# A two-layer transformer kernel: projection parts made by other engines, routing spaced, exponentials taken by halves of the queries

## The reference, cut to what matters

```python
x = x + attn_a(layernorm(x))     # causal softmax(q k / 4) v, one k and one v for all heads
x = x + ffn(layernorm(x))
x = x + attn_b(layernorm(x))     # causal softmax(q k / 4 + slope * distance) v
x = x + ffn(layernorm(x))

def ffn(x):
    shared = (silu(x @ sw1.T) * (x @ sw2.T)) @ sw3.T
    scores = sigmoid(x @ router_w.T)
    top = top_k(scores + expert_bias, 2)
    share = scores[top] / (scores[top].sum(-1) + 1e-9)
    routed = sum(share[e] * (silu(h1_e) * h2_e) @ w3[e].T for e in top)
    return shared + routed
```

## Time and profile before

| | us |
|---|---|
| median of 3 runs | 1129.21 |
| lowest and highest | 1126.43 to 1132.49 |
| the profiled execution, its own time | 1143.65 |
| span of the profiled execution (first to last instruction) | 1141.8 |
| PE busy (matmul) | 1035.0, 91% of the span |
| PEld busy | 656.1, 57% |
| DVE busy | 790.4, 69% |
| ACT busy | 591.4, 52% |
| POOL busy | 404.2, 35% |

### The profile page before, as it was taken

How to read it: one execution, slowest core, us unless ns; L and a number is a source line. 1 busy time by engine, 2 the same in 40 slices (tenths; PEclk the granted TensorE clock), 3 DMA queues, 4 the chain that set the end, 5 groups by cost and what they waited for, 6 DMA issues and landing times. The chain is left out here.

```text
span 1141.8 us, 20106 instructions
## 1 busy us (share of the span) xinstructions
PE 1035.0 (91%) x6848; PEld 656.1 (57%) x6848; DVE 790.4 (69%) x1584; ACT 591.4 (52%) x1258; POOL 404.2 (35%) x426
## 2 busy tenths in 40 slices
PE   4799999999998898999887999999999887989998
PEld 3433333333376788888775343434334776888877
DVE  7898788887366754448687978887873757544465
ACT  6317677777743335533253367776676333355332
POOL 3503632323535215345553002321235442163361
PEclk9859999999998999999899799999999988999999
DMA  4550111110033224533149423332211421245351
GB/s 132 148 84 17 36 40 35 36 40 27 25 106 139 66 84 145 132 109 94 46 137 184 81 46 61 69 62 57 57 27 27 144 96 57 74 144 140 111 159 54
DMA packets 65380, 94.99 MB, mean 83 GB/s; under 512 B 20575, under 2 KB 49183, under 8 KB 62929
## 3 DMA queue, kind: packets, MB, share of 16 engines
q1 hardware_dynamic: 44549, 52.28, 17.7%
q10 hardware_dynamic: 13820, 22.54, 7.3%
q0 software_dynamic: 6912, 18.88, 6.3%
HBM read 66.33 MB, written 26.67 MB: 81 GB/s over the span
## 5 line engine op out<-in xcount | busy, mean ns | idle before, releaser
L1200 ACT ACTIVATE pt<-st_ps 128x512 f32<-128x512 f32 (+3 forms) x768 | 327.4, 493 | 187.8 <-PE st_ps L846 112.2
L846 PE MATMUL st_ps<-qs,ks 99*128 99x512 bf16 (+7 forms) x768 | 243.0, 330 | 8.0 <-ACT pt L1200 5.6
L1439 DVE TENSOR_REDUCE mab<-su_ps 128x1 f32<-128x512 f32 (+2 forms) x288 | 181.5, 662 | 28.1 <-PE su_ps L826 19.9
L603 POOL TENSOR_SCALAR_AFFINE_SELECT pt<-pt 128x512 f32<-128x512 f32 x112 | 71.1, 635 | 341.5 <-ACT pt L1200 341.5
L864 PE MATMUL o_ps<-pt,vp 128*32 128x512 f32 (+3 forms) x1536 | 163.6, 498 | 1.9 <-POOL pt L603 1.0
L822 PE MATMUL su_ps<-ks,qs 96*128 96x512 bf16 (+5 forms) x448 | 159.0, 370 | 2.9 <-DVE mab L1439 1.6
L846 PEld LDWEIGHTS st_ps<-qs,ks 99*128 99x128 bf16 (+1 forms) x768 | 73.3, 98 | 113.2 <-ACT pt L1200 63.3
L680 POOL DMA_INDIRECT rows_in<-rows,source x80 | 76.3, 954 | 154.0 <-PE st_ps L1037 70.2
L1226 ACT CAST hh<-hf 128x512 fp32r<-128x512 f32 x64 | 39.7, 620 | 168.7 <-DVE hf L1640 160.9
L178 PE MATMUL st_ps<-xt_h,wu 128*128 128x512 f32 x256 | 103.5, 404 | 6.3 <-DVE xt_l L1364 3.7
L179 PE MATMUL st_ps<-xt_h,wu 128*128 128x512 f32 x256 | 102.4, 400 | 0.0
(11 more groups left out here) (220 smaller groups left out, 2132.7 us busy)
## 6 DMA issues: line engine op xcount, KB each, us to landing
wu_raw<-w_units_dram SPq DMA_DIRECT2D x32, 384.0 KB
outs<-rows_out ACTq DMA_DIRECT2D x40, 256.0 KB
qs<-q_parts ACTq DMA_DIRECT2D x60, 128.0 KB
q_parts<-hml SPq DMA_DIRECT2D x16, 384.0 KB, 3.3
wexp_raw<-w_units_dram SPq DMA_DIRECT2D x16, 384.0 KB, 6.6
qs<-q_parts SPq DMA_DIRECT2D x36, 128.0 KB
inv<-inverses SPq DMA_DIRECT2D x128, 32.0 KB, 1.8
rows<-xn SPq DMA_DIRECT2D x8, 512.0 KB, 6.3
```

The source lines that it names most:

```text
L603: pool.affine_select(block, block, [[0, 4], [1, P]], ALU.is_ge, 0.0, base=0, channel_multiplier=-1).then_inc(masked, 1)
L846: last = pe.matmul(bank[KM_BANKS[n % len(KM_BANKS)]][:, lo - CH * part:hi - CH * part], key_stack(l, s)(j)[0:rows, P * kt:P * kt + P], qs[ ...
L1200: act.activation(pt[:, kt % 2, j, lo:hi], bank[KM_BANKS[i % len(KM_BANKS)]][:, lo - CH * part:hi - CH * part], ACT.Exp, scale=1 / np.sqrt( ...
L1439: dve.tensor_reduce(to, bank[SU_BANKS[n % len(SU_BANKS)]][:, 0:share * width].rearrange("p (j k) -> p j k", j=share), AX.X, ALU.max).then_ ...
```

## The change

1. **Blocks of exponentials.** `QUADS` takes all four blocks of the first half of the queries first, then the eight of the second half. The division of the previous step's results on POOL stands once, behind kt 3, instead of in two parts behind kt 2 and kt 4; in the last step POOL's other jobs stand there too.
2. **Output projections.** In the last step they stand behind pieces 2, 5, ..., 23 instead of 10, 13, ..., 31, and those of the tiles 8 to 11 behind pieces 40, 42, 44 and 46 instead of behind the transposes after attention.
3. **Routing and searches.** The stages are spread over later items, the low parts of the two experts' weights go behind items 12 and 14.
4. **Projection parts.** ACT's float32 copy `yb` goes (32 rows of it stay for layer 0's keys and values); DVE subtracts the high part straight from PSUM, and the cast of the second part goes to ACT (`middle`). In layer 0 the transposes of a chunk stand inside the groups of the one ahead.
5. **Layer 1's last chunk.** All six groups of chunk 3, four splits among them, stand in the prelude, behind maxima 2, 5, ..., 17.
6. **Opening.** The filled part of `vp` is 128x1024 instead of 128x8192, and chunk 0's first rows are normalised right behind their own statistics.
7. **Between attention and feed forward.** DVE's order changes (the normalisation of chunk 2 ahead of the second division), and POOL's last weight split waits until all rows are normalised.

```diff
-ROUTE_BEHIND = {2: (0, 1), 3: (2, 3), 4: (4, 5), 8: (6,), 9: (7,)}
-FIND_BEHIND = {5: (0, 1), 6: (2, 3), 7: (4, 5)}
+ROUTE_BEHIND = {3: (0,), 4: (1,), 5: (2, 3), 6: (4, 5), 10: (6,), 11: (7,)}
+FIND_BEHIND = {7: (0, 1), 8: (2, 3), 9: (4, 5)}
-EXPERT_BEHIND = {4: 6, 6: 7}
+EXPERT_BEHIND = {12: 6, 14: 7}
...
-QUADS = [(kt, part) for kt in range(QT) for part in range(kt // HALF, 2)]
+QUADS = [(kt, 0) for kt in range(HALF)] + [(kt, 1) for kt in range(QT)]
...
-FC_BEHIND = {10 + 3 * t: t for t in range(QT)}
+FC_BEHIND = {**{2 + 3 * t: t for t in range(QT)}, **{40 + 2 * t: QT + t for t in range(HALF)}}
-INVERT_AT, DIVIDE_BEHIND = (6, 27), (2, 4)
+INVERT_AT, DIVIDE_BEHIND = (6, 27), 3
...
-FIRST_UNITS = {2: 4, 3: 8, 4: 12, 5: 16}
+FIRST_UNITS = {0: 2, 1: 5, 2: 8, 3: 11, 4: 14, 5: 17}
...
-                        elif s and kt in DIVIDE_BEHIND:
-                            divide(l, s - 1, DIVIDE_BEHIND.index(kt))
+                        elif s and kt == DIVIDE_BEHIND:
+                            divide(l, s - 1, 0)
...
-                if kt == 0:
+                if kt == 3:
                     split_unit(l, 0)
-                if kt == 1:
                     divide(l, STEPS - 2, 0)
-                if kt == 2:
                     split_unit(l, 1)
-                if kt == 3:
                     divide(l, STEPS - 2, 1)
-                    rstds(2 * l + 1, 0, 1)
-                if kt == 4:
-                    rstds(2 * l + 1, 1, 2)
+                    rstds(2 * l + 1, 0, 2)
 
...
+                rstds(2 * f + 1, 2, 3)
                 split_unit(f, 2)
-                rstds(2 * f + 1, 2, 4)
+                rstds(2 * f + 1, 3, 4)
+                pool.wait_ge(xn_done, TT * (2 * f + 2))
                 split_unit(f, 3)
...
-                transpose_chunk(0, 1)
-                pe.wait_ge(w_split, 2)
                 for c in range(NCH):
+                    if c == 0:
+                        pe.wait_ge(w_split, 2)
                     pe.wait_ge(xtl_done, KE * (c + 1))
-                    for m in range(3):
-                        qkv_group(0, c, m)
-
+                    qkv_group(0, c, 0)
+                    if c + 1 < NCH:
+                        transpose_chunk(0, c + 1)
+                    qkv_group(0, c, 1)
+                    qkv_group(0, c, 2)
                     n = qkv_index(0, c, 0)
-                    pe.wait_ge(evac_done, n + 1)
+                    pe.wait_ge(kv_copied, c + 1)
+                    pe.wait_ge(rest_done, split_index(0, c, 0) + 1)
                     for t in range(TC):
                         last = pe.transpose(bank[4 + n % 4][:, 32 * t:32 * t + 32],
-                                            yb[0:32, split_index(0, c, 0) % 2, P * t:P * t + P], ident[0:32, 0:32])
+                                            yb[0:32, c % 2, P * t:P * t + P], ident[0:32, 0:32])
                     last.then_inc(vt_done, 1)
-                    if c + 2 < NCH:
-                        transpose_chunk(0, c + 2)
 
...
                 transpose_chunk(p, 0)
                 transpose_chunk(p, 1)
-                for tt in range(QT, QT + HALF):
-                    output_projection(l, tt)
                 route(l, 0)
                 route(l, 1)
...
+                        last.then_inc(values_taken, 1)
+                    else:
+                        y = split_index(l, c, m)
+                        bias = {"bias": bias_a[:, m:m + 1]} if l == 0 else {}
+                        wait(act, parts_out[y % PBUFS], 16 * (y // PBUFS))
+                        act.activation(hml[:, y % PBUFS, 0, :], src, ACT.Identity, **bias).then_inc(high_done, 1)
+                        if kind == "kv":
+                            wait(act, vt_done, c - 1)
+                            act.activation(yb[0:32, c % 2, :], src[0:32, :], ACT.Identity, bias=bias_a[0:32, m:m + 1]).then_inc(kv_copied, 1)
+                            if c + 1 < NCH:
+                                x_hi(0, c + 1)
+                    if cast is not None:
+                        middle(cast)
+                    cast = y if kind != "v" else None
+                    if (l, c, m) == (1, 0, 5):
+                        x_hi(2, 2)
+                    if (l, c, m) == (1, 2, 1):
                         x_hi(2, 3)
+                if cast is not None:
+                    middle(cast)
 
+            def middle(y):
+                act.wait_ge(rest_done, y + 1)
+                act.copy(hml[:, y % PBUFS, 1, :], yr[:, y % 2, :]).then_inc(mid_done, 1)
 
...
-            act.activation(vp[:, :, :, :].rearrange("p t h d -> p (t h d)"), mhalf[:, 0:1].to_broadcast([P, TT * H * 32]),
-                           ACT.Identity, scale=-2.0).then_inc(ones_set, 1)
+            act.activation(vp[:, :, 0:H // 2, :].rearrange("p t (o j) d -> p t o j d", o=2)[:, :, :, 0, :],
+                           mhalf[:, 0:1].unsqueeze(2).unsqueeze(3).to_broadcast([P, TT, 2, 32]), ACT.Identity, scale=-2.0).then_inc(ones_set, 1)
...
-                dve.wait_ge(evac_done, qkv_index(l, c, m) + 1)
+                src, high = qkv_bank(qkv_index(l, c, m)), hml[:, y % PBUFS, 0, :]
                 dve.wait_ge(high_done, y + 1)
+                if l == 0 and m == 0:
+                    dve.wait_ge(kv_copied, c + 1)
                 wait(dve, parts_done, y - 1)
-                dve.tensor_tensor(yr[:, y % 2, :], yb[:, y % 2, :], hml[:, y % PBUFS, 0, :], ALU.subtract).then_inc(rest_done, 1)
-                dve.wait_ge(rest_done, y + 1)
-                dve.tensor_copy(hml[:, y % PBUFS, 1, :], yr[:, y % 2, :]).then_inc(mid_done, 1)
-            def split_chunk(l, c):
-                for m in range(SPLIT[l]):
-                    split(l, c, m)
                 if l == 0:
-                    n = qkv_index(l, c, 0)
-                    dve.wait_ge(vt_done, c + 1)
-                    src = bank[4 + n % 4][:, 0:32 * TC].rearrange("p (t m) -> p t m", m=32)[:, :, D:32]
-                    dve.tensor_copy(vp[:, TC * c:TC * c + TC, 0, 0:D], src)
-                    dve.tensor_copy(vp[:, TC * c:TC * c + TC, 4, D:32], src).then_inc(vc_done, 1)
+                    dve.scalar_tensor_tensor(yr[:, y % 2, :], src, bias_a[:, m:m + 1], high, ALU.add, ALU.subtract).then_inc(rest_done, 1)
+                else:
+                    dve.tensor_tensor(yr[:, y % 2, :], src, high, ALU.subtract).then_inc(rest_done, 1)
...
             def qkv_b():
+                split(1, 0, 0)
                 add_shared(0, 2)
-                split(1, 0, 0)
+                split(1, 0, 1)
                 stats(2, 2)
-                split(1, 0, 1)
+                split(1, 0, 2)
+                add_shared(0, 3)
+                split(1, 0, 3)
                 normalise(2, 2)
-                split(1, 0, 2)
-                split(1, 0, 3)
-                split_chunk(1, 1)
+                split(1, 1, 0)
+                stats(2, 3)
+                split(1, 1, 1)
+                split(1, 1, 2)
+                normalise(2, 3)
+                split(1, 1, 3)
                 lows(2, 2)
-                add_shared(0, 3)
-                stats(2, 3)
                 split(1, 2, 0)
-                normalise(2, 3)
                 split(1, 2, 1)
+                lows(2, 3)
                 split(1, 2, 2)
                 split(1, 2, 3)
-                lows(2, 3)
-                split(1, 3, 0)
-                split(1, 3, 1)
...
             def attention(l):
                 for u in range(NSU - 1):
-                    if l and u - 2 in (FIRST_UNITS[2], FIRST_UNITS[3]):
-                        split(1, 3, 2 if u - 2 == FIRST_UNITS[2] else 3)
+                    for m in range(SPLIT[1]):
...
                 stats(p, 1)
+                invert(step_no(l, STEPS - 1), 0)
                 normalise(p, 0)
-                invert(step_no(l, STEPS - 1), 0)
                 normalise(p, 1)
                 divide_last(l, 0)
+                add_projection(l, 4)
+                add_projection(l, 5)
+                stats(p, 2)
                 lows(p, 0)
                 invert(step_no(l, STEPS - 1), 1)
                 lows(p, 1)
-                add_projection(l, 4)
-                add_projection(l, 5)
-                stats(p, 2)
+                normalise(p, 2)
                 divide_last(l, 1)
                 hidden(l, 0)
-                normalise(p, 2)
                 hidden(l, 1)
                 add_projection(l, 6)
...
```

100 lines of the change are left out of this document (57 added, 43 removed).

## The result

The changed kernel takes 1145.97 us (median of 4 runs, 1144.12 to 1146.24) where the kernel before, in 4 runs beside it, takes 1130.84 (1126.43 to 1132.49): a ratio of 1.0137 with a 95% interval of 1.0103 to 1.0170. It is slower by 1.4%; the forecast was 1118.5, in a range of 1104 to 1132. A ratio leaves out a run that stands far above the others of its kernel (one of the four of experiment 15, 2411.68 us).

A forecast was written before the change was run, and what follows sets the result against it. PE was taken to bound the steps with maxima, with gains only in its gaps elsewhere. 14 + 6 - 11.1 - 9.2 - 3.5 - 7 = -10.8 us; -10.7 from the median 1129.21 gave 1118.5, range 1104 to 1132.

The forecast's parts named there:

- Blocks by halves, steps with maxima: Fourteen attention steps with maxima: exponentials' buffers wanted again sooner, 1.0 us lost a step, +14 us, bounds +4 to +27.
- the prediction's own sign: The prediction called itself wrong if the steps alone differ from +14 by over 10, or ACT holds up the projection.
- PE's own work per block: Attention steps: PE's work shared by a block's queries plus 128, 3.04 us for 512, 2.43 for 384, 1.83, 1.22.
- Rival (b): Attention steps: each of eight tight blocks costs 0.3 us or more, 2.3 a step, +42 instead of +20, 1140; chance 0.12.
- Last step: Last attention step of each layer: the buffer cycle sets the pace, projections mostly hidden; +3.0 us each, +6 together.
- Between: Between attention and feed forward: projections leave, 2.8 us a layer, and normalisation avoids POOL's weight work; -11.1, bounds -7 to -14.
- Routing: First feed-forward items: DVE's routing work moved to later items, -5.1 us in layer 0, -4.1 in layer 1; -9.2 together.
- rival (d): First items and projection: closing PE's gaps keeps the clock at 2.4 GHz, perhaps 7 us more gain, 1111; chance 0.08.
- Opening: Start to first scores: smaller fill on ACT and earlier first normalisation, 10.64 to about 7.9 us; -3.5, bounds -1 and -6.
- Which move with it: Opening: the rest of the chain to the first scores at 49.45, parts, stores and loads, moves with the first normalisation.
- Projection and prelude: Layer 1's projection and prelude: DVE loses casts, gain taken as nearly PE's 6.4 us of idle time; -7 us.
- The rule of the Trainium skill on VectorE's copies: Float32 SBUF copies run at 2x on VectorE, not with PSUM operands; if so here, projection gain some 5 us smaller.

The follow-up runs named there:

- experiment 15: Changed kernel, two buffers, with the old order of the blocks, old POOL divisions and projection places, low parts ahead of additions; ratio 0.9899 to the kernel before.
- Experiment 4: Changed kernel with a third buffer of exponentials for the second half of the queries, instruction order untouched; 1116.15 us, ratio 0.9881 to the kernel before.
- experiment 14: Kernel before with the third buffer for the second half of the queries, old order of the blocks; ratio 0.9900 to the kernel before.
- Experiment 2: Kernel before with the new order of the blocks alone; ratio 1.0292 to the kernel before, 33 us slower.
- experiment 11: Kernel of experiment 9 with the four projections behind the transposes and DVE's low parts ahead of their additions; ratio 0.9826 to the kernel before.
- experiment 12: Kernel of experiment 9 without POOL's wait for the normalised rows ahead of its last weight split; ratio 0.9895 to the kernel before.
- experiment 6: Kernel before with the new places of routing stages, searches and two experts' low parts alone; ratio 0.9888 to the kernel before, 11.7 us less.
- experiment 8: Kernel of experiment 7 with layer 0's opening reordered too: POOL's later roots behind last parts, DVE's chunk 0 splits earlier; 1117.64 us, ratio 0.9893.
- Experiment 7: Third-buffer kernel of experiment 4 with layer 1's projection reordered, POOL's first last parts ahead of roots and DVE's splits earlier; 1112.79 us, ratio 0.9844.
- experiment 9: Kernel of experiment 7 with two of chunk 3's groups and their splits back ahead of layer 1's prelude; 1108.09 us, ratio 0.9805 to the kernel before.
- experiments 3 and 10: Changed kernel with old block order and four projections behind the transposes, ratio 1.0098; kernel of experiment 9 with those four projections behind the transposes, 0.9889.

## Why the prediction was wrong

The sum failed by 25.9 us (-10.8 forecast, some +15 measured). By its own steps:

**Blocks by halves, steps with maxima: +14 forecast, +29.6 measured.** This step decided, and by the prediction's own sign (over 10 from +14) it failed. The mechanism was right: ACT waits for values at 8 places, and the cycle of a tight wide block is 3.14 to 3.16 us where I had 3.12. What failed is the other side of the comparison, "PE's own work per block". I spread the maxima evenly and got 3.04 for a block of 512. Experiment 4 shows 2.85, 3.07, 2.45 and 2.55: units are whole, and some wide blocks get few. So four wide gaps cost 12.32 - 10.92 = 1.4 us, where I had 0.24 for three. The pair at the end of a step costs 0.58, but did so before (experiment 14), and this I had misread too: that PE doesn't wait there was read from PE's idle time, which lists no wait for exponentials in layer 0's seven steps (0.30 us of idle time in a steady step, and 0.35 with the third buffer, when these 0.58 are gone). The stretch 78 to 287.6 that I divided by seven isn't the seven steps either: these run from 72.63 to 279.34. With both, a period pays 1.98 for two buffers against 0.58 in the old order, and 0.35 more since by halves it runs at 29.51 and not at 29.16 with three: 1.98 - 0.58 + 0.35 = 1.75, the measured difference of periods. The 0.35 is about the one wait of 0.30 that PE has for ACT's exponentials in the first half, which keeps its two buffers in experiment 4; under the old order with three (experiment 14) PE has no such wait in these steps. No run gives the first half a third buffer, so that this is the cause is likely and not shown. I had 0.7 for these two blocks.

The period is that of layer 0. Over the seven steps, the old order with three buffers takes 203.62 and 204.90 us and halves with three take 206.00 and 214.46: of the 29.6 us, 2.4 in layer 0 and 9.6 in layer 1 are left when the second half's reuse is gone, and some 18 are that reuse. Layer 1's 9.6 stay open. PE waits there for ACT for 5.7 us in 15 places, and under the old order not at all; the seven steps of layer 1 took 212.9 to 218.2 in the seven profiles by halves with three buffers, and 204.6 and 204.9 in the two of the old order. Rival (b), 2.3 a step, was the nearest to the truth, and I gave it 0.12. I had its evidence: PE stands in order, and a sum of small shortfalls has no slack to be paid from where PE is full.

**Last step: +6 forecast, +9.8 measured.** Experiment 2 has +2.0 from the blocks in each; the other 2.9 are the projections (3.0 by experiment 11), of which I had hidden all but 1.7.

**Between: -11.1 forecast, -12.6 measured.** The size is right. The move of the four projections takes 3.9 and 3.8 out of this stretch (experiment 11), but nearly all of it comes back in the last step: together it is worth 0.9 in layer 0 and nothing in layer 1. The normalisation beside POOL is real: 1.0 and 4.3 by experiment 12. These are 13.1 already, so nothing is left for DVE's new order by itself.

**Routing: -9.2 forecast, -12.6 to item 10 and -15.6 to item 15 measured;** alone -12.4 to item 15 (experiment 6). DVE was what the items waited for. The rise of the granted clock from 0.85 to 1.00 in this stretch, half of rival (d), is part of it: at 2.4 instead of 1.2 GHz PE's own work is shorter (busy 37.26 us with 197 matmuls before, 33.57 with 208 now), which my count of DVE's work left out. How much of the gain is the clock's no run separates. The Trainium skill ("TensorE: Matmul & The Clock Gate", Part 1) has idle gaps bring the lower clock. The traces agree: PE's longest gaps in this stretch of layer 0 were 3.65 and 2.60 us before, at a clock of 0.85, and are 1.75 and 1.41 now, at 1.00.

**Opening: -3.5 forecast, +0.5 measured,** which is no change: with this opening the first scores come at 49.5 to 50.1 us in the other profiles (experiment 8 aside, which changes it), with the old one at 49.5 to 49.8. The first normalisation starts at 8.29 us (10.64 before, 7.9 forecast). Nothing of it arrives at the first scores: PE waits 8.03 us for the stack (4.21 before), which comes from the last parts. "Which move with it" was the wrong step: the first last part starts at 24.15 us, 23.34 before, and the sixth ends at 36.5, 36.3 before. Why is argued only. POOL takes the roots of all four chunks ahead of its first last part and waits 3.75 us for the last chunk's statistics, but experiment 8, which moved these roots, changed other things with them and lost.

**Projection and prelude: -7 forecast, +3.5 measured.** DVE did lose its work (31.39 to 20.45 us busy), and POOL's parts take 1.17 instead of 1.55. But I bounded the gain by PE's idle time, and the stage ends with a chain: DVE's difference, ACT's cast, POOL's part, a store and a load. In it POOL first waited 11.02 us for statistics. Experiment 7 took 4.1 us off by order alone. In the prelude the two more groups cost 1.4 to 1.6 (experiment 9). The rule of the Trainium skill on VectorE's copies that the prediction weighed changed nothing: neither engine's load set this stage's end.

So four of six sizes lay outside their bounds, two of them with the wrong sign, and the one that decided was the cover I computed from an even spread instead of reading it.

## What to carry to other kernels

When a change brings the reuse of a buffer nearer, compare its cycle with the work that the waiting engine has between exactly these uses, block by block, and not with the average; on an engine that is full every shortfall is lost, and its idle time doesn't show it: of 1.75 us more in a step, PE's idle time showed 0.7. Only the distance between the same instructions, before and after, does. A shorter load of an engine is worth nothing where the stage ends with a chain through memory: follow the last transfer back to what it waited for first, and look at the order in which each engine serves that chain. A part of a change that is undone alone takes its companions with it (experiments 3 and 10), so undo these as well before it gets a price.

## What the runs showed of the hardware

- The normalisation of four tiles on DVE takes 1.38 us alone and 5.53 beside POOL's weight splits. In the trace of experiment 12 each of the four lasts about as long as the POOL instruction that it begins beside: 0.90, 2.00, 0.91 and 1.96 us beside 0.83, 1.84, 0.89 and 1.80.
- A POOL subtraction of 128x512 in the projection of layer 1 took 1.55 with DVE's cast beside it (which then took 1.28 instead of 0.43) and 1.17 with that cast on ACT.
- The stretch of items 16 to 31 of layer 0, in which POOL issues gathers, took 63.9 us in all profiles from three chips and 71.6 to 72.7 in all three from a fourth, whatever the kernel: the kernel before is at 1129 to 1130 us on the ones and at 1147 on the other. Over both layers two profiles differ there by 11 to 15 us, more than the whole effect that was forecast.
- PE's busy time in one step rose from 29.43 to 30.51 us, at full clock and with the same matmuls, when ACT held them up: in a stream of overlapping records, waits that are shorter than a record don't count as idle.
